# Graph convolution: four of eight scaled source pieces are made by GpSimd instead of VectorE

## What is computed

```python
def _ngcf_conv(x, W1, W2, src, dst, n_nodes):
    deg_out = jnp.clip(segment_sum(ones, src), 1.0)
    deg_in = jnp.clip(segment_sum(ones, dst), 1.0)
    norm = rsqrt(deg_out[src] * deg_in[dst])
    msg = (x[src] @ W1 + x[src] * x[dst] @ W2) * norm[:, None]
    return x @ W1 + segment_sum(msg, dst)

h = maximum(layernorm(x), 0)
out = x + conv(relu(conv(h, W1_1, W2_1)), W1_2, W2_2)
```

## Time and profile before

| | |
|---|---|
| Median of three executions | 479.75 us |
| The profiled execution | 477.81 us |
| its span, first to last instruction | 475.9 us |
| TensorE busy (matmul) | 461.0 us, 97% |
| VectorE busy | 415.5 us, 87% |
| ScalarE busy | 301.1 us, 63% |
| GpSimd busy | 152.8 us, 32% |
| Mean granted TensorE clock | 0.995 |

### The profile page before, as it was taken

One profiled execution on the slowest core, in us unless ns is written; L12 is line 12 of the kernel. 1 busy time (PEld: TensorE's weight loads), 2 busy tenths in 40 slices (PEclk: granted clock), 3 DMA queues, 4 the chain that ended last, 5 costly groups with the idle time before them and its releaser, 6 DMA issues.

```text
span 475.9 us, 20140 instructions
## 1 busy us (share of the span) xinstructions
PE 461.0 (97%) x8079; PEld 432.6 (91%) x8079; DVE 415.5 (87%) x1127; ACT 301.1 (63%) x799; POOL 152.8 (32%) x381
## 2 busy tenths in 40 slices
PE   5889999999999998999999999999999999999996
PEld 5778888888788888999999999999999999999996
DVE  6999999999999988889898998987888788888773
ACT  1399999999999994435453544434465555555551
POOL 3532524241627500444444455543111111111110
PEclk9999999999999999999999999999999999999999
DMA  3329513131303000001111111110011111111124
GB/s 73 92 51 151 95 26 82 26 78 20 83 4 68 1 3 8 3 14 26 28 27 26 26 23 26 26 26 8 9 26 24 29 26 25 24 26 25 31 55 100
DMA packets 50104, 18.07 MB, mean 38 GB/s; under 512 B 46336, under 2 KB 48688, under 8 KB 50013
## 3 DMA queue, kind: packets, MB, share of 16 engines
q1 hardware_dynamic: 48623, 14.63, 16.1%
q0 software_dynamic: 672, 2.01, 1.5%
q10 hardware_dynamic: 718, 0.16, 0.2%
HBM read 6.28 MB, written 4.19 MB: 22 GB/s over the span
## 4 chain that ended last, share of the span: by engine, by line
PE 77%; DVE 16%; issue 3%; DMA 2%; ACT 1%; DVEq 0%; ACTq 0%
PE diff L1192 34%; PE iota_bank L1192 18%; PE slab L1093 13%; DVE los L785 10%; PE diff L1075 5%; PE diff L1143 2%; DVE stats L794 1%; DMA prev_i<-in_dst_dram 1%; PE diff L1044 1%; PE diff L1156 1%; DMA work<-mixed 1%; ACT hots L1243 1%; PE diff L1189 1%; PE slab L1192 1%; PE iota_bank L1156 1%
## 5 line engine op out<-in xcount | busy, mean ns | idle before, releaser
L785 DVE TENSOR_TENSOR los<-mixed,iota_bank 128x5120 bf16<-128x5120 bf16 x49 | 136.9, 2807 | 1.0 <-PE slab L1093 0.9
L1093 PEld LDWEIGHTS slab<-hots,los 128*128 128x128 bf16 x2352 | 115.4, 97 | 14.3 <-ACT words L1251 1.2
L1093 PE MATMUL slab<-hots,los 128*128 128x98 fp8e5 x2352 | 121.2, 208 | 0.5 <-DVE los L785 0.4
L1243 ACT ACTIVATE hots<-diff 128x784 f16<-128x784 f32 x147 | 118.8, 853 | 4.4 <-PE diff L1075 4.4
L1192 PE MATMUL diff<-late,mixed 128*128 128x128 f16 x1567 | 95.2, 219 | 0.0
L659 POOL TENSOR_TENSOR work<-work,h 128x64 f32<-128x64 f32 x97 | 31.3, 323 | 193.5 <-DVE work L929 193.5
L1192 PE MATMUL diff<-los,mixed 128*128 128x129 f16 x1470 | 90.1, 220 | 0.0
L1192 PEld LDWEIGHTS diff<-late,mixed 128*128 128x128 fp8e4 x1567 | 89.6, 98 | 0.1
L1192 PEld LDWEIGHTS diff<-los,mixed 128*128 128x128 fp8e4 x1470 | 84.8, 98 | 0.0
L1075 PE MATMUL diff<-select,mixed 80*128 80x392 f16 x294 | 65.3, 329 | 2.3 <-ACT hots L1243 2.3
L837 DVE TENSOR_SCALAR mixed<-words 128x400 int32<-128x400 int32 x192 | 66.2, 373 | 0.0
(11 more groups left out here) (213 smaller groups left out, 563.1 us busy)
## 6 DMA issues: line engine op xcount, KB each, us to landing
x_sb<-in_x_dram SPq DMA_DIRECT2D x4, 384.0 KB
rows_table<-rows SPq DMA_DIRECT2D x6, 252.0 KB, 2.6
mixed<-rows_table SPq DMA_DIRECT2D x18, 84.0 KB, 3.0
work<-mixed SPq DMA_TRANSPOSE x82, 2.3
out_dram<-x_sb SPq DMA_DIRECT2D x8, 128.0 KB
los<-in_dst_dram SPq DMA_DIRECT2D x1, 750.0 KB
p_table<-p_rows_sb SPq DMA_DIRECT2D x24, 28.0 KB
p_table<-p_rows_sb SPq DMA_DIRECT2D x24, 7.0 KB
```

The costliest lines, as they stand in the source:

```text
L785: nc.vector.tensor_tensor(out=los[:, b % LOS_RING].rearrange("e s (v t) -> e s v t", t=2), in0=key, in1=val, op=ALU.is_equal).then_inc(los ...
L1093: ins = nc.tensor.matmul(to, los[:, u // 2 % LOS_RING, u % 2 * ULOWS + low], pairs, start=(step == 0), stop=(step == USTEPS - 1), skip_gro ...
L1243: nc.scalar.activation(bass.AP(to.tensor, to.offset, [to.ap[0], [step, 2], [STEPS * HPITCH, 8], [1, BLOCKS]]), diff[m % 2][:, :, 0:HALF].r ...
```

## The change

GpSimd makes the last four scaled pieces (blocks 21 to 49), ahead of its wait for `rdo_kept`, and counts them on a semaphore of its own, on which ScalarE waits for these pieces. VectorE makes the first four and all low parts, in the order scaled 0, scaled 1, high 0, low 0, low 1, scaled 2, scaled 3, low 2 to low 7.

```diff
+    pool_scaled = sem("pool_scaled")
...
+    POOL_PIECES = 4
...
+            pool.wait_ge(rdo_ready, 1)
+            pool.wait_ge(normed, BLOCKS // PIECE)
+            for q0, q1 in PIECES[POOL_PIECES:]:
+                nc.gpsimd.tensor_tensor(out=scaled[:, q0:q1], in0=h[:, q0:q1],
+                                        in1=rdo_sc0[:, q0:q1].unsqueeze(2).to_broadcast([128, q1 - q0, D]),
+                                        op=ALU.mult).then_inc(pool_scaled, 1)
             pool.wait_ge(rdo_kept, 1)
...
             low_piece(0)
             low_piece(1)
             scaled_piece(2)
-            for i in range(3, len(PIECES)):
-                scaled_piece(i)
-                low_piece(i - 1)
-            low_piece(len(PIECES) - 1)
+            scaled_piece(3)
+            for i in range(2, len(PIECES)):
+                low_piece(i)
...
             for i, (q0, q1) in enumerate(PIECES):
-                act.wait_ge(scaled_ready, i + 1)
+                if i < POOL_PIECES:
+                    act.wait_ge(scaled_ready, i + 1)
+                else:
+                    act.wait_ge(pool_scaled, i + 1 - POOL_PIECES)
```

## The result

The kernel after took 481.90 us (median of six executions, 481.35 to 482.36), the kernel before 479.79 (479.25 to 480.43): ratio 1.0044, interval 1.0033 to 1.0055, so 1.6 to 2.6 us slower. Forecast were 482.6 us, between 480.8 and 484.4.

What follows compares the result with a forecast made beforehand. Low piece 2's arrival, set by VectorE's chain, was taken to bound the stretch, with TensorE setting the pace behind it. Delay +2.55 us and clock +0.3 us gave +2.85 us on the 479.75 us median: 482.6 us, range 480.8 to 484.4.

Steps and rivals of the forecast that it cites:

- The path: Between build and first convolution units, only low piece 2's arrival counts; relieving VectorE of 2.1 us behind it is worth 0.
- The turns: GpSimd's products and VectorE's two-input pieces alternate by whole instructions ahead of low piece 2: +2.55 us, chance 0.62.
- My schedule: Alternating instructions after the reciprocal: scaled 1 ends 182.71, low 1 184.80, scaled 2 186.07 instead of 183.52 us.
- a GpSimd that keeps the port: Rival: GpSimd runs its four products in a row while scaled 1 waits; 483.7 to 485.1 us, chance 0.14.
- a VectorE that keeps it: Rival: GpSimd gets in only beside L904 and in the wait for ScalarE; +0.9 us, 480.6 us, chance 0.12.
- No blocking: Rival: reads of 448 elements mix freely, VectorE's chain stays as it is; 479.75 us, chance 0.10.
- The price of a product: GpSimd's turn for 448 elements beside VectorE's chain, priced from the trace's rows: 0.79 us.
- The larger figure: Skill page's estimate for a 448-element GpSimd turn: 0.97 us, four turns 0.7 us more, term +3.3 us.
- The clock: TensorE's longer pauses may lower its granted clock, an even chance; half of 0.6 us taken, +0.3 us, bounds 0 and 1.7.
- the third pause that I forecast: TensorE was to pause 1.9, 0.7 and 1.2 us, the last ahead of step 2.
- The sum: Low piece 2's delay and TensorE's clock together: +2.85 us, added to the median for 482.6 us.
- the wider range: For 8 in 10, whole kernel between 480.8 and 484.4 us, reaching into the cases where one engine keeps the port.

Runs made afterwards that it cites:

- e3: Kernel after, with GpSimd making only scaled piece 7 and VectorE the other seven; 478.74 us, ratio 1.0021 to the kernel before.
- s2: Kernel after, with GpSimd making only pieces 6 and 7 and 66 instead of 34 filler matmuls behind the build; 478.42 us, ratio 1.0015 to the kernel before.
- r2: Kernel after, with more filler matmuls in TensorE's three pauses to hold its clock; 481.83 us, ratio 1.0047 to the kernel before.
- e1: Kernel after, without GpSimd's four products and ScalarE's waits for them, nobody making pieces 4 to 7; 477.58 us, ratio 0.9995 to the kernel before.
- s1: Kernel before, with four added GpSimd products that nobody uses, a repeat in a later group; 480.30 us, ratio 1.0064 to the kernel before.
- r3: Kernel after, with GpSimd's four products replaced by memsets of the same 448 columns; 479.18 us, ratio 0.9994 to the kernel before.
- r4: Kernel after, with GpSimd making only pieces 6 and 7 and VectorE the other six; 480.90 us, ratio 1.0029 to the kernel before.
- the two of the contention alone: Kernel before plus four GpSimd products that nobody uses, run twice: 481.91 us, ratio 1.0093, and again as s1.
- r1: Kernel after, unchanged, measured again in the second group; 482.26 us, ratio 1.0052 to the kernel before.
- s3: Kernel before, without GpSimd pieces, ScalarE making high part 0, VectorE's pieces reordered, 6 fillers instead of 12; 477.28 us, ratio 0.9996.
- e2: Kernel after, with GpSimd starting its four products only when low piece 2 is there; 478.11 us, ratio 1.0008 to the kernel before.

## Why the prediction was right

**The path.** Right: low piece 2 sets the stage. Moved by 0.74, 1.09 or 2.56 us it moved the stage by 0.74 (e3: 12.22 us), 1.09 (s2) and 2.52 (r2), and taking 2.1 us of work from VectorE behind it gave 0.05 (e1).

**The turns.** Right to a few hundredths. My schedule, moved by the 1.69 us that the reciprocal started later, has scaled 1 ending at 184.40, low 1 at 186.49 and scaled 2 at 187.76; the records end at 184.40 (182.97 + 1.43), 186.49 (184.70 + 1.79) and 187.76 (186.41 and the longest L895 of this profile, 1.353 us). e3 shows the first turn alone, s1 all four without the rest of the change. Of the rivals, a GpSimd that keeps the port would have put all four products ahead of scaled 1, and a VectorE that keeps it would have left scaled 1 at its length; the records of both are against it. "No blocking" falls with every run that has products. That the exclusion is between whole instructions for 448 elements too was inferred from 64; it held. The section of the Trainium skill, "SBUF — State Buffer", "Who interferes with whom", says that a VectorE instruction with two SBUF inputs collides with a GpSimd one that reads SBUF, not with one that only writes it, and that one with a single SBUF input does so only in what the page calls 2-port performance modes. The trace agrees on the first two (scaled and low pieces against products, against memsets in r3), and L904 with its single input wasn't held (0.34 us, r4). A single input is no safe sign all the same: the unpack of the earlier trace rows has one too and was held for the rest of GpSimd's product. In which mode it ran, no row shows.

**The price of a product.** 0.79 us per turn from the rows was right. The larger figure by the Trainium skill, "GPSIMD Engine Reference", section "Elementwise — side-by-side cycle accounting", would have put low piece 2 another 0.7 us later, which the 6.56 us rule out.

**The clock.** The term of 0.3 us was a compromise between 0 and 0.6 and the weakest step; that the sum came near the stage by it is partly luck. The clock fell in both profiles of the kernel after and cost 0.47 and 0.75 us there (against r2); in the two of the contention alone it cost 0.1 or less. What differs is where the fall lay: in s1 from about 183.8 to 187.2 us, and step 2 began at 187.38; in r1 from about 187.8 to 191.2, and step 2 began at 189.55. That it can fall, and what it costs when its rest lies on step 2, was right. I had read that it fell once in the trace before; it falls a second time in the last microsecond there, when TensorE has no work left, which changes nothing. What I left out is that it slows the fillers too: the third pause that I forecast, 1.2 us ahead of step 2, isn't in the profile after, since the 12 fillers at half pace filled it (in r1 0.55 us of it are left), and in r4 they delayed step 2.

**The sum.** The stage grew by 2.99 us in the first profile and 3.27 in the second; 2.85 were forecast. The times grew by 2.1 (1.6 to 2.6) and 2.7 us (1.7 to 3.3). Both intervals hold the 2.5 to 2.6 us by which the stage grew where the clock cost next to nothing (r2, s1). But the first ends below the 2.85 us of the sum, and 481.90 us lies just under the 482.0 to 484.0 that I had given for the turns alone: the sum was 0.7 us too high there, and only the wider range holds it. It also ends below the growth of the profiled stage. Layer 1 took nothing of the delay up, 135.36 to 135.39 us in the profiles of the kernel after and of the kernel before alike. Layer 2 was 0.82 us shorter in both profiles of the kernel after, but it was as short in s3 (139.24 us), where GpSimd makes no piece and VectorE all eight; so whether the delay shortens it, or the one profile before happened to have a long one, stays open.

## What to carry to other kernels

Work taken from a busy engine is worth something only ahead of the wait that sets the stage. Before a two-input elementwise operation goes to GpSimd, look at what VectorE does in the same microseconds: if that reads two SBUF tensors, both will take turns, and each turn on the critical chain adds up to most of one GpSimd instruction (here 0.74 us for the first product of 0.94, 0.35 for the second, which lay partly beside L904, and 2.56 for all four). If it must go there, start it behind the critical piece (e2: one wait, 0.3 us in the times instead of 2 to 3), and size the fillers that keep TensorE's clock up for the new pause, or they end up on the path.

## What was not expected

- With two products the profiled stage was 2.22 us longer, and 1.13 of these were a clock that fell after a pause of 2.04 us and ran 12 filler matmuls in 1.49 us instead of 0.83 (r4, s2). In e3, with a pause of 1.69 us, it didn't fall.
- The build of the same code took 157.7 to 157.8 us in two groups of runs and 159.2 to 159.9 in the third and in the first profile of the kernel after: 1.5 us that have nothing to do with the kernel. Two spans compared across groups would have put them on the change.
- Four GpSimd memsets of 448 columns took 1.71 us together and disturbed nothing.
